# Two attention layers and two expert layers on one core: the engine orders of the second attention, the way out of the first, and the front of the expert layer are re-arranged

## What is computed

```python
x = x + attn_a(layernorm(x))    # 2 x 2048 tokens, 128 wide
x = x + ffn(layernorm(x))       # 16 experts, top 256 tokens each
x = x + attn_b(layernorm(x))    # linear attention, 16 heads of 8
x = x + ffn(layernorm(x))       # the same expert weights again
# attn_a: complex recurrence s = a*s + a*u along time; h = V s + xc; out = real(h) @ w_out.T
# attn_b (phi = elu+1): num = q . running sum of k v^T ; den = q . running sum of k
#         out = (num / max(den, 1e-6)) @ W_out.T
# ffn: logits = rmsnorm(x) @ router.T + b; each expert takes its 256 highest tokens,
#      gelu MLP, scattered back with gates
```

## Time and profile before

| | us |
|---|---|
| median of 3 runs | 712.15 (710.78 to 713.48) |
| the profiled execution | 713.5, span 711.8 |

### The profile page before, as it was taken

One profiled execution on the slowest core, in us unless ns is written; L12 is line 12 of the kernel. 1 busy time (PEld: TensorE's weight loads), 2 busy tenths in 40 slices (PEclk: granted clock), 3 DMA queues, 4 the chain that ended last, 5 costly groups with the idle time before them and its releaser, 6 DMA issues.

```text
span 711.8 us, 7588 instructions
## 1 busy us (share of the span) xinstructions
PE 390.4 (55%) x2094; PEld 277.2 (39%) x2094; DVE 422.9 (59%) x1220; ACT 219.4 (31%) x530; POOL 360.4 (51%) x390
## 2 busy tenths in 40 slices
PE   4896766095331786683035656766753316877550
PEld 4554435073110575573012233433321104766540
DVE  6787999985877222222447877788868773221210
ACT  2567000026741132232033343333157510422110
POOL 5046950003101768787308876678831016678853
PEclk9999878587555699898555777777675555999985
DMA  5960000007203223335838888789552032233322
GB/s 143 355 252 1 0 1 0 0 1 206 60 29 44 56 36 43 44 39 67 207 39 127 135 132 101 105 113 123 74 178 88 30 44 51 33 43 44 44 23 18
DMA packets 67400, 55.70 MB, mean 78 GB/s; under 512 B 18017, under 2 KB 55521, under 8 KB 66081
## 3 DMA queue, kind: packets, MB, share of 16 engines
q1 hardware_dynamic: 47744, 44.63, 29.9%
q0 software_dynamic: 11392, 9.05, 9.5%
q10 hardware_dynamic: 8224, 1.57, 1.5%
HBM read 22.73 MB, written 15.73 MB: 54 GB/s over the span
## 4 chain that ended last, share of the span: by engine, by line
DVE 26%; PE 22%; POOL 16%; issue 15%; DMA 10%; ACT 4%; SPq 2%; another core or an unknown queue 2%; DVEq 1%; ACTq 0%; POOLq 0%
DVE arena L1220 10%; POOL out L537 6%; POOL acc L537 5%; POOL arena L524 3%; DVE arena L1225 3%; PE ps L1156 3%; DVE tk L1225 3%; DMA acc<-arena,idx 2%; PE ps L939 2%; DMA out<-arena,idx 2%; PE ps L979 2%; DMA arena<-arena 2%; DVE arena L1620 2%; PE ps L1182 2%
## 5 line engine op out<-in xcount | busy, mean ns | idle before, releaser
L1220 DVE TENSOR_TENSOR arena<-ps,arena 128x256 f32<-128x256 f32 (+1 forms) x84 | 35.1, 430 | 152.6 <-DMA out<-arena,idx 68.5
L766 ACT ACTIVATE arena<-ps,b 128x256 f32<-128x256 f32 x128 | 50.0, 475 | 141.7 <-PE ps L1095 105.1
L600 POOL TENSOR_TENSOR tb<-arena 128x512 f32<-128x512 f32 x64 | 71.1, 1124 | 24.6 <-DVE arena L1620 21.6
L1095 PE MATMUL ps<-arena,f1w 128*128 128x256 f32 x256 | 73.9, 440 | 15.4 <-DVE arena L1224 12.1
L524 POOL DMA_INDIRECT arena<-tab,idx x64 | 62.8, 981 | 34.3 <-issue 18.9
L1105 PE MATMUL ps<-f2w,arena 128*128 128x128 f32 x512 | 65.3, 280 | 6.4 <-issue 3.5
L1105 PEld LDWEIGHTS ps<-f2w,arena 128*128 128x128 f32 x512 | 64.5, 197 | 9.7 <-issue 6.5
L1095 PEld LDWEIGHTS ps<-arena,f1w 128*128 128x128 f32 x256 | 54.3, 223 | 25.7 <-DVE arena L1224 14.2
L537 POOL DMA_INDIRECT out<-arena,idx x32 | 50.9, 1591 | 25.4 <-issue 15.6
L537 POOL DMA_INDIRECT acc<-arena,idx x32 | 50.6, 1581 | 13.6 <-issue 7.6
L1220 DVE TENSOR_TENSOR arena<-arena 128x256 f32<-128x256 f32 (+21 forms) x107 | 56.0, 558 | 2.2
(11 more groups left out here) (264 smaller groups left out, 931.4 us busy)
## 6 DMA issues: line engine op xcount, KB each, us to landing
arena<-arena SPq DMA_DIRECT2D x64, 256.0 KB, 7.2
f1w<-in_f1T SPq DMA_DIRECT2D x4, 1024.0 KB, 12.0
f2w<-in_f2T SPq DMA_DIRECT2D x4, 1024.0 KB, 14.0
tab<-tb SPq DMA_DIRECT2D x8, 512.0 KB, 3.3
acc<-tb SPq DMA_DIRECT2D x8, 256.0 KB, 18.8
arena<-in_f2b SPq DMA_DIRECT2D x2, 1024.0 KB, 5.8
acc<-xs SPq DMA_DIRECT2D x8, 256.0 KB, 6.1
xs<-acc SPq DMA_DIRECT2D x8, 256.0 KB, 5.3
```

The source lines that it names most:

```text
L600: pool.tensor_tensor(by_pairs(QS[:, i, :]), sums_for(i, r), by_pairs(qn[:, r, :]), ALU.mult).then_inc(qs_ready, 1)
L766: last = nc.scalar.activation(hT[:, e % 2, t, :], ps[:, 2 * (e % 2) + t // 2, (t % 2) * CAP:(t % 2 + 1) * CAP], ACT.Gelu, bias=b1[:, e, t: ...
L1095: last = nc.tensor.matmul(ps[:, 2 * (e % 2) + t // 2, (t % 2) * CAP:(t % 2 + 1) * CAP], f1w[:, e, t * P:(t + 1) * P], xeT[:, e % 2, :], st ...
L1220: return nc.vector.tensor_tensor(o, a, b, op)
```

## The change

1. Way out: each batch is a product of its own, 64 rows by 128 columns into its own bank (`BY_QUARTER` gives the order of groups). Two such products take the place of one of 128 rows by 256 columns. `ao_ready` is released per quarter (two banks) and no more per bank.
2. Expert front of feed(0): all eight groups are transposed first, then `spread_scale` (with a wait for four kept groups), then the even and the odd routes. The dummy Exp stands behind the factor copy.
3. Second attention, TensorE: the order becomes `to_xT(n+1)`, `project_out(n-2)`, `project_q(n+1)`, `sum_own(n)`, `project_k(n+1)`, `numerator(n-1,0)`, `project_v(n+1)`, `spread_reciprocals(n-1)`, `numerator_own(n-1)`, `numerator(n-1,1)`, the rest as it was.
4. Second attention, ScalarE: q and k exps, then v; the transposed group is kept after `keep_k_even`; `keep_raw` goes last. In the last round a dummy Sqrt loads that table.
5. The first ten rounds of the search are a loop with one pass on VectorE, in both expert layers.

```diff
             for n in range(2 * NK):
-                act.wait_ge(ao_ready, n + 1)
-                nc.scalar.activation(xrows[:, :, 2 * n:2 * n + 2, :], ps[:, n, :].rearrange("p (t b d) -> p b t d", t=2, b=NB),
+                g = BY_QUARTER[n]
+                act.wait_ge(ao_ready, n // NB + 1)
+                nc.scalar.activation(xs[:, g * TPG:(g + 1) * TPG, :].rearrange("p t d -> p (t d)"), ps[:, n, :],
                                      ACT.Copy).then_inc(x1_ready, 1)
...
-                nc.scalar.activation(nrm[:, 3:4], ident[:, 0:1], ACT.Exp)
+                if f:
+                    nc.scalar.activation(nrm[:, 3:4], ident[:, 0:1], ACT.Exp)
                 act.wait_ge(logit_prod if f else r_spread, f + 1)
                 nc.scalar.activation(L, ps[:, 0 if f else 3, :], ACT.Copy).then_inc(factor_kept, 1)
+                if f == 0:
+                    nc.scalar.activation(nrm[:, 3:4], ident[:, 0:1], ACT.Exp)
...
+            keep_normed(0)
+            keep_v(0)
             for n in range(NG + 1):
                 if n < NG:
-                    act.wait_ge(transposed, NG + n + 1)
-                    nc.scalar.activation(xT[:, n * GW:(n + 1) * GW], ps[:, 5, :], ACT.Copy).then_inc(xT_ready, 1)
-                if n < NG:
-                    keep_v(n)
                     exp_min(q_prod, 6, exq, q_ready, q_neg, q_exp, n)
                     exp_min(k_prod, 5, exk, k_ready, k_neg, k_exp, n)
-                if n >= 3:
-                    keep_raw(1, n - 3)
+                    if n:
+                        keep_v(n)
+                else:
+                    nc.scalar.activation(nrm[:, 3:4], ident[:, 0:1], ACT.Sqrt)
                 if n + 2 < NG:
                     norm(n + 2)
                 if n >= 2:
                     keep_spread(n - 2)
                 if n < NG:
                     keep_k_even(n)
+                if n + 1 < NG:
+                    keep_normed(n + 1)
                 if n >= 1:
                     spread(n - 1)
+                if n >= 3:
+                    keep_raw(1, n - 3)
...
+            def way_out(m, t, i, values):
+
+                for b in range(NB):
+                    rows = slice(64 * b, 64 * b + 64)
+                    last = nc.tensor.matmul(ps[:, 2 * m + b, t * D:(t + 1) * D], values[rows, :], MB[rows, i, b, :],
+                                            start=(i == 2 and t == 0), stop=(i == 1), skip_group_check=True)
+                return last
...
-            for n in range(2 * NK):
-                pe.wait_ge(s_ready, n // 2 + 1)
-                for t in range(2):
-                    at = (2 * n + t) * P
+            for m in range(NK):
+                pe.wait_ge(s_ready, m + 1)
+                for t in range(TPG):
+                    at = (TPG * m + t) * P
                     for i in range(2):
-                        last = way_out(n, t, i, SS[:, i, at:at + P])
+                        last = way_out(m, t, i, SS[:, i, at:at + P])
                 last.then_inc(ao_ready, 1)
...
                 if f == 0:
-                    for n in range(NG - 1):
+                    for n in range(NG):
                         transpose_raw(f, n)
+                    spread_scale(f)
                     pe.wait_ge(rawT_kept, NG - 2)
                     for g in range(0, NG, 2):
                         route(g)
-                    transpose_raw(f, NG - 1)
-                    spread_scale(f)
                     pe.wait_ge(rawT_kept, NG)
...
             for n in range(NG + 2):
-                if n < NG:
-                    sum_own(n)
-                if 1 <= n <= NG:
-                    numerator(n - 1, 0)
+                if n + 1 < NG:
+                    to_xT(n + 1)
                 if n >= 2:
                     project_out(n - 2)
                 if n + 1 < NG:
-                    to_xT(n + 1)
-                    project_v(n + 1)
                     project_q(n + 1)
+                if n < NG:
+                    sum_own(n)
+                if n + 1 < NG:
                     project_k(n + 1)
                 if 1 <= n <= NG:
+                    numerator(n - 1, 0)
+                if n + 1 < NG:
+                    project_v(n + 1)
+                if 1 <= n <= NG:
+                    spread_reciprocals(n - 1)
                     numerator_own(n - 1)
                     numerator(n - 1, 1)
-                    spread_reciprocals(n - 1)
...
-                for j in range(BITS):
-                    bit(j, j)
+                with dve.Fori(0, BITS, BITS) as r:
+                    for j in range(BITS):
+                        bit(r + j, j)
```

More of the change, by code:

```diff
@@ L206, in build @@
         POOL_TILES, EARLY_TILES, EXP_AT = 8, 4, 10
+        BY_QUARTER = [b * NK + m for m in range(NK) for b in range(NB)]
         raw_T, rawT_kept, r_wide, r_spread = sem("raw_T"), sem("rawT_kept"), sem("r_wide"), sem("r_spread")
@@ L868, in transpose_raw @@
                 for t in range(TPG):
-                    j = n * TPG + t if f else (t // 2) * (NT // NB) + 2 * n + t % 2
+                    j = (n if f else BY_QUARTER[n]) * TPG + t
                     last = nc.tensor.transpose(ps[:, 1 if f else n, t * P:(t + 1) * P], xs[:, j, :], ident[:, :])
@@ L976, in _ @@
             pe.wait_ge(raw_ready, 2 * NK)
-            def way_out(n, t, i, lhs):
-                return nc.tensor.matmul(ps[:, n, t * 2 * D:(t + 1) * 2 * D], lhs, MB[:, i, :, :].rearrange("p b d -> p (b d)"),
-                                        start=(i == 2 and t == 0), stop=(i == 1), skip_group_check=True)
-            for n in range(2 * NK):
-                for t in range(2):
-                    at = (2 * n + t) * P + 1
-                    way_out(n, t, 2, XC[:, 0, at:at + P])
-                    nc.tensor.matmul(ps[:, n, t * 2 * D:(t + 1) * 2 * D], ident[:, :], xrows[:, :, 2 * n + t, :],
+            def way_out(m, t, i, values):
[6 more added lines that the diff above has]
+                for t in range(TPG):
+                    at = (TPG * m + t) * P + 1
+                    way_out(m, t, 2, XC[:, 0, at:at + P])
+                for b in range(NB):
+                    g = b * NK + m
+                    nc.tensor.matmul(ps[:, 2 * m + b, :], ident[:, :], xs[:, g * TPG:(g + 1) * TPG, :].rearrange("p t d -> p (t d)"),
                                      start=False, stop=False, skip_group_check=True)
-            for n in range(2 * NK):
-                pe.wait_ge(s_ready, n // 2 + 1)
-                for t in range(2):
-                    at = (2 * n + t) * P
+            for m in range(NK):
+                pe.wait_ge(s_ready, m + 1)
+                for t in range(TPG):
+                    at = (TPG * m + t) * P
                     for i in range(2):
-                        last = way_out(n, t, i, SS[:, i, at:at + P])
+                        last = way_out(m, t, i, SS[:, i, at:at + P])
                 last.then_inc(ao_ready, 1)
@@ L1375, in _ @@
                 dve.wait_ge(x1_ready, n + 1)
-                for j in (2 * n, 2 * n + 1, NT // 2 + 2 * n, NT // 2 + 2 * n + 1):
-                    V.did(nc.vector.bn_stats(bst[:, j, :], xs[:, j, :]))
+                stats(BY_QUARTER[n])
             def feed(f):
```

13 lines of the change are left out of this document (7 added, 6 removed).

## The result

The median of the kernel after is 689.91 us (689.62 to 692.55, 4 runs); the kernel before took 711.46 (710.49 to 713.48, 4 runs) beside it. The ratio is 0.9702, 95% interval 0.9669 to 0.9735, so 21.5 us are gone. The profiled execution took 692.55 us, the slowest of the four, with a span of 690.8 against 711.8. One execution of the kernel with half the stream, further down, ran in a slower state of the chip (727.26 us at a granted clock of 0.543) and is left out of that median.

What follows compares the result with a forecast made beforehand. No single engine: TensorE bound the way out, ScalarE's factor copy the front, a three-engine loop the second attention. Terms 5.1 + 1.5 + 12 + 1.5 + 0.4 = 20.5 off 712.15 gave 691.65 us; eight-in-ten range 687 to 703.

Steps and rivals of the forecast that it cites:

- the forecast's own range: Whole kernel: 687 to 699 us if the forecast's mechanisms hold, chance 0.58.
- Way out, 5.1 us: Products after the first attention's scan: batches run side by side, TensorE ends near 154.2 instead of 160.0; 5.1 us gained.
- Rows queue: Rival, way out: the paired products don't run side by side; 697.4 us, chance 0.17.
- Front, 1.5 us: Expert front: factor copy freed of the table load, gap between even and odd routes closed; 0.9 to 2.9, taken 1.5 us.
- the 164 named as the mark: Sign for the way out: VectorE's product with the factors starts near 164.
- Loop, 12 us: Second attention: waits before `take_q` and `divide` go, transfers of spread v set the step; 10.9 to 13.4, taken 12 us.
- Late v: Rival, second attention: v kept near +10 or stream empties each step, loop gains half; 697.7 us, chance 0.13.
- the starved stream: Rival, second attention: v kept so late that the transfer stream starts from empty; slower, 719.7 us at y = 18, chance 0.04.
- The formula for late v: Second attention: with v kept y us after `take_z`, a step lasts (y + 22.6)/2 us.
- End of the loop and Sqrt table, 1.9 us: After the loop: `divide(7)` waits for the numerator alone, 1.5 us; Sqrt table loaded ahead, 0.4 us.
- Search rounds, 0: Both expert layers' searches: 0.07 us a round won, loop entries cost it back; -0.5 to +0.5, taken as nothing.

Runs made afterwards that it cites:

- the kernel with half the stream: Kernel after, with each spread-of-v transfer from step 1 on moving half the columns: 684.35 us, ratio 0.9629 to before.
- ScalarE's list alone: Kernel before with only ScalarE's new order of the second attention (with the Sqrt table), TensorE's order old: 708.03 us, ratio 0.9965.
- three other profiles with the same attention code: Kernels with the attention part alone, batches one after the other, half of the statistics; `take_z(0)` to first count 139.3, 140.0 and 140.7 us.

## Why the prediction was right, and where it was off

The forecast was 691.7 us, the time 689.9, inside the forecast's own range. Faster by more than 0.5% was right, and no rival came true. That the total is so near is in part luck: the way out gave less than its term, and the loop more. The sum of 20.5 us was near the 21.5 measured; its terms were not all so.

- **Way out, 5.1 us: the term was too large, 2.8 in the profile, and 4.0 with some 1.5 either way by the run of that part alone.** The step that failed is where I let the end of TensorE set the end of the stage. The pairs work, and the products took the time I gave them. Of the 32 `bn_stats`, 0.196 us each, 28 ran while TensorE was still at its products in before; now 10 do, and the other 22 come after it. The sum asked what would be late next for ScalarE's copies alone, and not for VectorE.
- **Rows queue: false.** A pair costs 0.129 us at 2.4 GHz with what lies around it. The price of this rival was too low: with the batches one after the other the time was 9.0 us above after, not 5.7, because the clock stayed at 1.2 GHz. The Trainium skill ("TensorE: Matmul & The Clock Gate", LDWEIGHTS) lets a load go by its columns whatever its rows; by that alone the loads would have been the bound. The Trainium skill ("TensorE: Matmul & The Clock Gate", Part 3 on packing small matmuls) has tiles on different rows run together; the trace agrees, 2.06 us for 32 passes.
- **Front, 1.5 us: 1.9 in the profile**, inside 0.9 to 2.9. Alone it gives 3.4 by the median and 2.8 in the profile: the prediction named the risk that routes fall into the slow clock, and with the new way out they partly do, 2.80 us for 1.93, and up to 3.64 in other profiles. VectorE's product with the factors started at 163.94, near the 164 named as the mark, but only because the start phase was 2 us shorter in this profile; behind the first product it is 22.0, where the mark meant 20.1.
- **Loop, 12 us: 14.0, beyond the 13.4 of its upper end.** Steps 2 to 6 gave 93.49 - 79.63 = 13.9. The mechanism is as told: transposes ahead of `take_z`, v kept at +6.85 for the +7.1, both of VectorE's waits gone, the stream next. What was mis-sized is the stream's pace: 12 stands for steps of 16.3 us, and steps 2 to 6 took 15.93 in the mean, which is 1.99 a transfer. SyncE's issues in after give nearly the same:

```profile
399.64 86.77 SPq L403 DMA_DIRECT2D arena<-arena  x43
```

  That is 2.02 us a transfer, with the pause in it that is told below. The landings' 1.97 of the prediction was nearer than the issues' 2.06, and steps of 16.0, which the prediction had beside it, would have given 13.4. Late v and the starved stream are false for this kernel. The formula for late v fits ScalarE's list alone (17.0 for 17.1), where the stream is all that is left to wait for; with `sum_own` at the head it falls short (16.3 for 17.42), because another wait stands beside it.
- **End of the loop and Sqrt table, 1.9 us: half of the mechanism right, and a loss left out.** 2.7 and 0.5 were won where I put them. All of the 2.7 is the early spread of the reciprocals; `project_out(6)`, to which the prediction gave up to 1.6 of it, adds nothing. In the profiled execution 3.1 were lost ahead of them, as VectorE has caught up with the last transfers. I counted the end as if the loop's speed-up left it alone. In after nothing stayed of the gain. In the three other profiles with the same attention code loop and end together are 1.1 to 2.5 us shorter. In after SyncE's queue shows two issues in 5.74 us, which take about 4 elsewhere:

```profile
475.39 5.74 SPq L403 DMA_DIRECT2D arena<-arena  x2
```

  This execution is also the slowest of the four, 2.6 us above their median. So it is likely that the kernel's usual execution keeps 1 to 2.5 us of this gain. What makes the pause is open.
- **Search rounds, 0: right.** VectorE waits 0.17 in every round of after, where the earlier trace rows has 0.24 in the straight ones, so the mechanism is there. The search took 0.2 and 0.8 us less in the profile, and 0.1 and 0.4 less with the part alone, whose time can't be told from none.

## What to carry to other kernels

When an engine that ends a stage is made faster, sum up for every other engine of the stage what work it has left from the moment it is free; here VectorE's statistics took back 1.8 of 4.6 us, and TensorE's new idle time slowed its next products. In a list that an engine works off in order, a wait at the head is paid by all that stands behind it, and by engines that wait to reuse a buffer: look for both, since the second is found in no wait of the engine that is moved. A loop brought down to its transfer stream should be counted with its last step, because part of the wait for the last transfers can show behind the loop; and a stage that differs by 3 us between profiles of the same code needs more than one profile.

## What the runs showed of the hardware

- Products of two batches on different halves of the rows, issued in turn, start 3 to 7 ns apart, and the next pair some 0.21 us later at 1.2 GHz and 0.11 at 2.4. Issued one half after the other, single passes start 0.213 us apart at 1.2 GHz.
- TensorE's clock stayed at 1.2 GHz through 22.8 us in which its products and loads were never idle, when these used 64 rows one after the other. In pairs, or with whole-height passes, it was at 2.4 GHz 3.6 to 5.3 us after the first product, in all thirteen other profiles.
- The scale's spread (four products) and 16 routes took 1.08 and 2.80 us behind 3.9 us of idle TensorE (up to 3.64 for the routes in other profiles), and 0.63 and 1.93 behind 1.4 or 2.0.
- A group of eight products in the start phase took 1.94 us in some profiles and 3.27 to 3.38 in others, by the clock that was granted. A profile of this kernel can therefore be 2 us off before the changed code begins.
- In after, the next `take_z` follows the landing of a step's last transfer by 3.05 to 3.17 us in all seven steps, and from step 2 on a step of eight transfers of 256 KB each lasted 15.93 us in the mean.
